# Layer 0's last results ahead of layer 1's first edges, two maxima earlier, the flag later, and extra transposes in the first slots

## The reference

```python
# layer 0: attention over a row, layer 2 the same with biases and elu
h = x @ W.T
e = leaky_relu(s_i + t_j, 0.2);  e = where(adj == 0, NEG, e)
out = softmax(e, axis=-1) @ h
# layer 1: softmax over a column (axis=1), then elu
att = softmax(where(adj > 0, leaky_relu(s1_i + s2_j, 0.2), NEG), axis=1)
out = elu(att @ h)
# layer 3: four relations (adj == 1 .. 4), y = sum_r (adj == r) @ x @ W_r + bias
```

## Time and profile before

| | us |
|---|---|
| median of 3 runs | 470.44 (469.98 to 471.45) |
| the profiled execution | 470.86 |
| its span in the trace | 469.1 |
| PE busy | 378.9 (81%) |
| DVE busy | 375.9 (80%) |
| ACT busy | 315.8 (67%) |
| POOL busy | 290.5 (62%) |

### The profile page before, as it was taken

How to read it: one execution, slowest core, us unless ns; L and a number is a source line. 1 busy time by engine, 2 the same in 40 slices (tenths; PEclk the granted TensorE clock), 3 DMA queues, 4 the chain that set the end, 5 groups by cost and what they waited for, 6 DMA issues and landing times. The chain is left out here.

```text
span 469.1 us, 9311 instructions
## 1 busy us (share of the span) xinstructions
PE 378.9 (81%) x2818; PEld 337.8 (72%) x2825; DVE 375.9 (80%) x1414; ACT 315.8 (67%) x805; POOL 290.5 (62%) x425
## 2 busy tenths in 40 slices
PE   2789998998666779778697787899999959888870
PEld 2689998997666779678696676899999855455440
DVE  0167999999866899999999855598889997888862
ACT  1467999999534475565555655487778747787864
POOL 3236888887443545354453565478787886878882
PEclk9799999999777999899998899799999999999985
DMA  5998662000000000000000000000000000011122
GB/s 156 222 249 223 121 132 47 2 1 1 2 1 2 0 0 2 1 1 2 0 2 0 2 2 1 1 1 1 1 1 2 3 0 1 21 65 52 67 76 86
DMA packets 8757, 18.21 MB, mean 39 GB/s; under 512 B 1280, under 2 KB 2560, under 8 KB 8704
## 3 DMA queue, kind: packets, MB, share of 16 engines
q0 software_dynamic: 2304, 8.39, 9.4%
q1 hardware_dynamic: 2976, 4.52, 2.9%
q10 hardware_dynamic: 3424, 4.66, 2.8%
HBM read 21.76 MB, written 4.19 MB: 55 GB/s over the span
## 5 line engine op out<-in xcount | busy, mean ns | idle before, releaser
L461 PE MATMUL o_ps<-h_scaled,PT 128*128 128x129 f32 (+1 forms) x1536 | 193.8, 288 | 17.1 <-DVE y L953 14.2
L461 PEld LDWEIGHTS o_ps<-h_scaled,PT 128*128 128x128 f32 x1536 | 188.8, 204 | 18.5 <-issue 14.9
L669 ACT ACTIVATE X<-y,offset,rstd 128x128 f32<-128x128 f32 x256 | 104.9, 482 | 38.9 <-POOL offset L270 38.7
L901 DVE SCALAR_TENSOR_TENSOR PT<-rows_ps,factors,MT 128x512 f32<-128x512 f32 x128 | 88.8, 737 | 0.8 <-PE rows_ps L448 0.6
L403 PE MATMUL h_ps<-wx,xT 128*128 128x130 f32 x384 | 66.7, 314 | 27.9 <-DVE smax L856 26.9
L403 PEld LDWEIGHTS h_ps<-wx,xT 128*128 128x128 f32 x384 | 56.5, 211 | 38.3 <-issue 37.2
L261 POOL TENSOR_TENSOR rstd<-var_eps,neg_half 128x4 f32<-128x4 f32 x64 | 66.4, 1038 | 5.0
L973 DVE BATCH_NORM_STATS2 stats<-y 128x6 f32<-128x128 f32 x256 | 56.0, 281 | 7.0 <-DVE y L967 0.5
L276 POOL TENSOR_TENSOR elu_exp<-elu_exp,X 128x512 f32<-128x512 f32 x32 | 40.7, 1272 | 18.8 <-ACT elu_exp L663 18.5
L251 POOL TENSOR_TENSOR h_scaled<-hx,factors 128x516 f32<-128x516 f32 x32 | 33.6, 1050 | 24.7 <-PE o_ps L461 14.8
L227 POOL TENSOR_TENSOR mean_term<-h_mean,empty_row 128x512 f32<-128x512 f32 x32 | 38.2, 1192 | 16.9 <-DVE residual L953 15.3
(11 more groups left out here) (98 smaller groups left out, 664.6 us busy)
## 6 DMA issues: line engine op xcount, KB each, us to landing
MT<-adj_by_j POOLq DMA_DIRECT2D x16, 512.0 KB, 8.7
X<-x SPq DMA_DIRECT2D x16, 256.0 KB, 6.0
out<-X ACTq DMA_DIRECT2D x16, 256.0 KB, 2.0
w_rel<-w SPq DMA_DIRECT2D x1, 256.0 KB, 3.1
w_back<-w_by_output ACTq DMA_DIRECT2D x1, 192.0 KB, 3.1
wx<-w_by_input ACTq DMA_DIRECT2D x1, 192.0 KB, 5.9
bias<-b ACTq DMA_DIRECT2D x1, 64.0 KB, 4.5
bias<-b SPq DMA_DIRECT2D x1, 64.0 KB, 8.4
```

Of the source, the lines that this page charges most:

```text
L461: last = pe.matmul(o_ps[it.b][:, ic, first:1 + D], PT[:, it.b, jc, ic * P:(ic + 1) * P], h_scaled[:, it.b, jc, first:1 + D], start=(jc == ...
L669: last = act.activation(X[:, g, c, :], y[:, b, c, :], ACT.Identity, bias=offset[:, b, c:c + 1], scale=rstd[:, b, c:c + 1])
L901: dve.scalar_tensor_tensor(out=PT[:, it.b, c, :], in0=rows_ps[:], scalar=factors[:, it.b, 1, c:c + 1], in1=m, op0=ALU.max, op1=ALU.mult, * ...
```

## The change

The diff does six things.

1. PE transposes the identity into `o_ps[0]`, which nothing reads: 24 times before it waits for the weights, 4 times after the small weight products, and in slots -4 to -1 three times before `spread_max`, three times before `project` and four times after it.
2. On DVE, `take_out` of a layer 0 item n-2 moves ahead of `edges`. That concerns slots 15, 16 and 17.
3. `take_max` of items 32 and 33 moves from the head of slots 30 and 31 into slots 29 and 30, ahead of `add_elu`.
4. `split_bias2` leaves DVE's slot 8. Five of its steps run on POOL at the end of slot 24, and three copies of one row each on ACT in slot 26.
5. The flag's steps move into the relation layer, DVE slots 54, 57 and 58, PE slot 56, with `smax_ps` in place of `xT_ps`.
6. With that, PE's slot 18 transposes item 22 at its usual place.

```diff
+FLAG_SLOT = G * LAYERS + 6
+            def split_bias2():
+                pool.wait_ge(sem("b2_a"), 1)
+                pool.wait_ge(sem("b_in"), B_IN)
+                pool.tensor_tensor(bias2[:, D:D + 2], b2_a[:, :], ab2_sb[:, :], ALU.add).then_inc(sem("bias2"), 1)
+                pool.wait_ge(sem("bias2"), 1)
+                pool.tensor_copy(bias2_hi[:, :], bias2[:, :]).then_inc(sem("bias2"), 1)
...
+                if n == G + 8:
+                    split_bias2()
...
+            def keep_busy(times):
+                for _ in range(times):
+                    pe.transpose(o_ps[0][:, 0, 0:P], ident[:], ident[:])
+            pe.wait_ge(sem("ident"), 1)
+            keep_busy(24)
             pe.wait_ge(sem("w_in"), W_IN)
...
-            pe.wait_ge(sem("ident"), 1)
+            keep_busy(4)
...
-                if at(4) and n != G + 2:
+                if at(4):
                     next_transpose(at(4))
+                if n < 0:
+                    keep_busy(3)
                 if at(2):
                     spread_max(at(2))
                 if at(1):
                     spread_rows(at(1))
-                if n == G + 2:
-                    pe.wait_ge(sem("flag_own"), 1)
-                    pe.wait_ge(sem("xT"), at(3).done)
-                    pe.transpose(xT_ps[:, 0:P], flag_own[:, 0:1].broadcast_to([P, P]), ident[:])\
-                        .then_inc(sem("flag_ps"), 1)
-                    pe.wait_ge(sem("flag_max"), 1)
-                    next_transpose(at(4))
+                if n < 0:
+                    keep_busy(3)
                 if at(3):
                     project(at(3))
+                if n < 0:
+                    keep_busy(4)
...
+                if n == FLAG_SLOT + 2:
+                    pe.wait_ge(sem("flag_own"), 1)
+                    pe.transpose(smax_ps, flag_own[:, 0:1].broadcast_to([P, P]), ident[:])\
+                        .then_inc(sem("flag_ps"), 1)
...
+                if n == G + 10:
+                    act.wait_ge(sem("bias2"), 5)
+                    act.copy(bias2_parts[0:1, :], bias2_hi[0:1, :])
+                    act.copy(bias2_parts[32:33, :], bias2_mid[32:33, :])
+                    act.copy(bias2_parts[64:65, :], bias2_low[64:65, :]).then_inc(sem("bias2_parts"), 1)
...
-                if n == 8:
-                    split_bias2()
                 if at(-1) and at(-1).l in (0, 2):
                     row_sums(at(-1))
-                if at(2) and not (at(2).l == 1 and at(0).l == 1):
+                if at(2) and not (at(0) and at(0).l == 1):
                     take_max(at(2))
                 if at(-1) and at(-1).l in (0, 2):
                     row_factors(at(-1))
+                if at(-2) and at(-2).l == 0:
+                    take_out(at(-2))
                 if at(1) and at(1).l == 1:
                     edges(at(1))
...
-                if at(-2) and at(-2).l == 0:
-                    take_out(at(-2))
...
-                if at(3) and at(3).l == 1 and at(1).l == 1:
+                if at(3) and at(1) and at(1).l == 1:
                     take_max(at(3))
...
-                if n == G + 1:
-                    dve.wait_ge(sem("flag_sum"), G)
-                    dve.tensor_reduce(flag_own[:, 0:1], flag_sum[:, :, 0], AX.X, ALU.max).then_inc(sem("flag_own"), 1)
...
+                if n == FLAG_SLOT:
+                    dve.wait_ge(sem("flag_sum"), G)
+                    dve.tensor_reduce(flag_own[:, 0:1], flag_sum[:, :, 0], AX.X, ALU.max).then_inc(sem("flag_own"), 1)
+                if n == FLAG_SLOT + 3:
+                    dve.wait_ge(sem("flag_ps"), 1)
+                    dve.tensor_reduce(flag_own[:, 1:2], smax_ps, AX.X, ALU.max).then_inc(sem("flag_max"), 1)
+                if n == FLAG_SLOT + 4:
+                    dve.wait_ge(sem("flag_max"), 1)
+                    dve.tensor_scalar(flag_int[:, :], flag_own[:, 1:2], 0.25 * C * N, None, ALU.is_gt)\
+                        .then_inc(sem("flag"), 1)
```

More of the change, by code:

```diff
@@ L117, in build @@
         bias2_parts = sb("bias2_parts", [P, 130], BF16)
+        bias2_low = sb("bias2_low", [P, 130], BF16)
         rank_one = sb("rank_one", [P, 2, P], BF16)
@@ L277, in elu_low @@
                     .then_inc(sem("elu_low"), 1)
+            def split_bias2():
[4 more added lines that the diff above has]
+                pool.tensor_copy(bias2_hi[:, :], bias2[:, :]).then_inc(sem("bias2"), 1)
+                pool.wait_ge(sem("bias2"), 2)
+                pool.tensor_tensor(bias2_rest[:, :], bias2[:, :], bias2_hi[:, :], ALU.subtract)\
+                    .then_inc(sem("bias2"), 1)
+                pool.wait_ge(sem("bias2"), 3)
+                pool.tensor_copy(bias2_mid[:, :], bias2_rest[:, :]).then_inc(sem("bias2"), 1)
+                pool.wait_ge(sem("bias2"), 4)
+                pool.tensor_tensor(bias2_low[:, :], bias2_rest[:, :], bias2_mid[:, :], ALU.subtract)\
+                    .then_inc(sem("bias2"), 1)
             def attention_slot(at, n):
@@ L829, in _ @@
             dve.memset(hx[:, :, :, 0:1], 1.0).then_inc(sem("ones"), 1)
[L831 to L839, removed]
-                    .then_inc(sem("bias2"), 1)
-                dve.wait_ge(sem("bias2"), 3)
-                dve.tensor_copy(bias2_mid[:, :], bias2_rest[:, :]).then_inc(sem("bias2"), 1)
-                dve.wait_ge(sem("bias2"), 4)
-                dve.tensor_copy(bias2_parts[32:33, :], bias2_mid[32:33, :])
-                dve.tensor_tensor(bias2_parts[64:65, :], bias2_rest[64:65, :], bias2_mid[64:65, :], ALU.subtract)\
-                    .then_inc(sem("bias2_parts"), 1)
             def own_max(it):
@@ L1036, in attention_slot @@
                     aggregate(at(-1))
-                if n == G + 1:
-                    dve.wait_ge(sem("flag_sum"), G)
-                    dve.tensor_reduce(flag_own[:, 0:1], flag_sum[:, :, 0], AX.X, ALU.max).then_inc(sem("flag_own"), 1)
-                    dve.wait_ge(sem("flag_ps"), 1)
-                    dve.tensor_reduce(flag_own[:, 1:2], xT_ps[:, 0:P], AX.X, ALU.max).then_inc(sem("flag_max"), 1)
-                    dve.wait_ge(sem("flag_max"), 1)
-                    dve.tensor_scalar(flag_int[:, :], flag_own[:, 1:2], 0.25 * C * N, None, ALU.is_gt)\
-                        .then_inc(sem("flag"), 1)
             def relation_slot(at, n):
```

## The result

The changed kernel took 454.74 us as the median of four runs (450.75, 454.10, 455.37, 455.75); the kernel before took 470.94 beside it. The ratio is 0.9639, with a 95% interval of 0.9574 to 0.9703. The profiled execution took 455.75 us with a span of 454.0, against a span of 469.1 before. The forecast was 454.8. A second set of four runs (the experiment "The changed kernel again") had a median of 451.40 against 470.40.

What follows compares the result with a forecast made beforehand. Bound: DVE, busy only 29.22 of 41 us between the layers, waiting 11.0 us in a ring with PE. Terms 10.7 + 1.4 - 0.3 + 1.4 + 0 + 2.5 = 15.7 gave 454.8 us; range 452 to 457.5, wider 451.5 to 459.5.

Steps and rivals of the forecast that it cites:

- Start: Slots -4 to -1: identity transposes raise PE's clock, 4.4 us gained less 1.7 for added ones and 0.2 for handoffs: 2.5.
- Split: Bias split out of DVE's slot 8: 1.4 us back; five POOL steps at the end of slot 24 cost 0.3.
- Slot 14: Layer 0's slot 14: not among the prediction's steps, so no gain forecast there.
- Slots 15 to 17: Between the layers, `take_out` ahead of `edges`: 11.0 us of waits, -0.5 rows, +0.6 flag steps, -0.4 port, 10.7 gained.
- The flag: Three DVE steps moved to the relation layer cost 0.6 us, hidden by DVE's idle 0.94: 0, at worst 0.6.
- the ring: Slots 15 to 17: DVE's `edges` delay `take_out`, PE's attend waits for it, DVE waits for the maximum behind: 7.2 us.
- Maxima: Items 32 and 33: earlier maximum lets `project` start 2 us earlier, removing DVE's 1.40 us wait for `hx`: 1.4 gained.
- A: Slots -4 and -3: clock not up, transposes in the way; start costs 1.3 us instead of gaining 2.5: 458.6, chance 0.13.
- D: Layer 0's dense slots: PE stays at 1.2 GHz, 4.1 us per slot, four slots eat the 15.7; chance 0.02.
- B: Slots 15 to 17 and near 24: DVE steps blocked by POOL at the shared port, 3.0 us more: 457.8, chance 0.14.
- C: Slots 15 to 17: moved `take_out` waits for `x_new` or `residual`, the 10.7 us fall to 0.6: 464.9, chance 0.04.
- E: Slots 29 and 30: early maximum makes DVE wait for PE's attend, 1.4 us lost and 2 more: 458.2, chance 0.07.

Runs made afterwards that it cites:

- the experiment with the first 28 alone: The changed kernel without the identity transposes inside slots -4 to -1, keeping the first 24 and next 4: median 453.03 us, ratio 0.9674.
- the direct experiment: The changed kernel with the bias split back on DVE in slot 8, POOL and ACT free of it: median 455.55 us, ratio 0.9719.
- the residuals alone: The kernel before with only `take_out` of layer 0's last results moved ahead of layer 1's `edges`: median 459.72 us, ratio 0.9782.
- the pair with the copies first: The changed kernel with ACT copying h and xT ahead of the normalization in slots 31 to 33, with early maxima 443.72 us, with late 445.45.
- the one with late maxima: The changed kernel with ACT's copies ahead of the normalization in slots 31 to 33 and the maxima's conditions as before: median 445.45 us, ratio 0.9495.

## Why the prediction was right, and where it wasn't

The sum was right to 0.6 us (15.1 measured in the profiled pair, 15.7 forecast), but not because every term was. The medians of the two sets were 16.2 and 19.0 us apart, so that closeness is partly the choice of the pair.

- **Start, 2.5 forecast, 1.58 measured** (over all traces, the first attend came at 27.3 in the mean of the eight with the full set of added transposes and the load of X as it was, and at 28.6 in that of the four without them: 1.3). The clock did what I said: the weights' products took 0.83 us, not 1.44, and all X transposes 0.60 to 0.66. The step that failed is the next limit. I followed ACT and PE and did not look at who loads the fifth block of X:

```profile
1.54 5.38 PE L400 MATMUL o_ps<-ident 128*128 128x128 f32 x24 [1.54 <-POOL ident L208]
7.82 0.83 PE L407 MATMUL xT_ps<-a_cols,w_back 128*128 128x2 f32 x6 [0.90 <-DMA wx<-w_by_input]
...
24.82 0.63 PE L415 MATMUL xT_ps<-ident,X 128*128 128x128 f32 x4 [2.51 <-DMA X<-x]
```

  SP issues that block only when the mask of graph 1, the second one, has landed (`mask_in1`). The 1.7 us that I charged for transposes inside the slots fell into this wait; no gain of theirs shows at the first attend either, by the experiment with the first 28 alone. The 1.7 was also added up wrongly: its items, 0.3, 0.7, 0.35, 0.35 and 0.3, make 2.0, so that the net should have read 2.2 and the forecast 455.1.
- **Split, 1.4 - 0.3 forecast.** Slots 7 to 9 gave 1.37, as said. I had not asked what the pause in slot 8 gave others: with it gone ACT sets the pace, slots 9 to 11 take 6.07 instead of 5.95, and 0.41 comes back. On POOL the five steps took 1.65 us together, against my 2.2, but two small POOL steps behind them, beside DVE's work, took 0.58 and 0.53 instead of 0.20, and from the edges of slot 20 to those of slot 26 the lead fell by 0.46, against 0.3. Net 0.5 in this pair of traces, 0.1 in the direct experiment, not 1.1.
- **Slot 14, nothing forecast, 1.6 measured.** The condition of the moved lines also holds in slot 14, where no edges stand; the description of the change names only slots 15 to 17. I had the row for it, and read it only as a price for other slots.
- **Slots 15 to 17, 10.7 forecast for the order, 11.7 measured** (15.86 at the edges of slot 20 less the 4.16 of attend 14; 12.4 from the edges of slot 15 to those of slot 18). The mechanism is shown: attends of slots 15 and 17 in 3.81 us, no wait of DVE for the maximum, one of 0.2 for the rows. I had left 0.5 for the rows and 0.4 for the port, and neither came. But the 11.7 holds the flag too. With the flag in its old place the order gave 9.4 (11.03 - 1.60), so for the order alone the 10.7, or 10.1 without the 0.6 for the flag's steps, was too much.
- **The flag, 0 forecast, 3.65 measured** by taking it back out of the changed kernel, 2.3 by the comparison with the residuals alone. This is the step that failed most. I priced its three steps on DVE (0.6) and looked for who hides them in their new place. I did not price what PE has behind the flag in the old one: X transposes, projection and attend, held back behind two waits for DVE. While `take_out` held the ring up, this was hidden; with the ring shortened it was next. In the relation layer the flag costs nothing that the trace shows: the lead stays between 14.69 and 14.88 through its slots, as forecast.
- **Maxima, 1.4 forecast.** They gave 1.5 to 1.9 in the pair with the copies first, where they also spared the attend of slot 30 a fall of the clock, which my term didn't have. The 1.40 us of idle time ahead of `own_max` of item 33 is gone, as forecast, but the lead of the profiled pair shows only 0.15 of it behind slot 35, because the clock fell twice there in the changed kernel's execution.
- **Rivals.** A and D: the clock was high from 7.8 us on. B: the small DVE steps of slots 15 to 17 took 0.22 to 0.29; among them a neighbour on POOL showed only in slot 14, to the good, and the 0.58 and 0.53 of POOL's steps behind the split are the only ones that came anew near slot 24. C: `take_out` waits for nothing. E: DVE does wait 3.63 us in slot 31, but for ACT's `hx`, and the kernel before has that wait too, 3.61 us in the same slot.

The misses had both signs: +1.6 in slot 14 and +1.0 in slots 15 to 20, against -0.9 at the start, -0.6 around the split, -1.3 behind slot 30 and -0.4 in slots 44 and later, -0.6 in all. The total was right in part by luck. Of the eight runs of the changed kernel four lie in the forecast's own range of 452 to 457.5 and five in the wider one of 451.5 to 459.5; three, 450.75 to 450.93, lie just below both. The one of these that was profiled was spared a fall of the clock that no term had priced.

## What to carry to other kernels

When a wait is moved or removed, list for every engine what is queued behind it in the old place too, because a step that was hidden by the stall becomes the next stall. Price a part by taking it back out of the new kernel, not only by adding it to the old one. Look in each engine's order for an instruction that waits for a long chain while others' input is ready behind it; one line that took the copies ahead of the normalization was worth about half of what the change gained, with no work removed. A pause of an engine is to be asked twice, for its own length and for the clock at which the work behind it runs.

## What the runs showed of the hardware that I had not expected

- The clock behind equal pauses differs between executions of one kernel. After idle times of 3.27 and 3.18 us PE ran at 0.54 and 0.57 of full speed for 7 and 8 us; in another execution, after 3.28 and 3.20 us, the first fall was over before the attend (3.79 us instead of 4.86) and the second didn't come. This is 4.1 of the 4.8 us between the two profiled executions (450.93 and 455.75 us); the other runs have no trace. Pauses of 1.44 us lowered nothing in any slot of the kernel with the first 28 transposes, but in the kernel before, the X transposes behind equal pauses of 1.44 us took 0.66 us once and 1.11 us once. Ahead of the transposes of slot 0, 2.51 us of idle time left them at 0.63 us in the changed kernel, while 1.96 us put them at 1.09 in the kernel with the added transposes alone and 2.21 us at 1.07 in the one with late maxima. So the length of the pause alone doesn't decide; what does stays open.
- 24 transposes of the identity while the weights were loading raised the clock by the weights' products (0.83 to 0.93 us against 1.44) and took 4.2 to 5.4 us. In two of the ten traces that have them, PE was at 1.2 GHz again behind these products (X transposes of 1.06 us) after idle times of 1.35 and 1.92 us ahead of them.
- With pauses of over 3 us gone, the work from attend 31 to attend 35 ran at a granted clock of 1.00 (251.47 to 278.44 us); the changed kernel had 0.83 and 0.95 for the same work in its two traces, the kernel before 0.91. Over the fixed stretch from 248 to 300 us, which holds different slots in each kernel, it is 1.00, 0.87, 0.97 and 0.88.
- A [128 x 4] step on DVE took 0.68 and 1.08 us beside two POOL steps of 1.05 and 1.04, and 0.22 without them: three to five times its price for having a neighbour.
